# A transformer block on one core: products with the values issued for two attention steps together, and a third buffer of exponentials

## The reference

```python
c6 = silu(c) @ Wc + bc                     # shift, scale, gate for each half
xm = modulate(ln(x), sh_msa, sc_msa)
q, k, v = xm @ Wq + bq, xm @ Wk + bk, xm @ Wv + bv     # split into 16 heads
w = softmax(q / 16 @ k^T)                  # 512 x 512 per head
x = x + g_msa * ((w @ v) @ Wo + bo)
h = gelu(modulate(ln(x), sh_mlp, sc_mlp) @ W1 + b1)    # exact gelu
x = x + g_mlp * (h @ W2 + b2)
```

## Time and profile before

| | |
|---|---|
| median of three runs | 863.87 us (856.36 to 866.10) |
| span of the profiled execution | 857.3 us; its own time is not listed beside it |
| mean granted TensorE clock | 0.906 |
| TensorE matmuls busy | 725.0 us, 85% |
| VectorE busy | 582.5 us, 68% |
| ScalarE busy | 384.3 us, 45% |
| GpSimd busy | 222.2 us, 26% |
| maxima of the score blocks (L895) | 335.9 us, 512 times |
| exponentials (L497) | 247.9 us, 256 times |
| score blocks (L594) | 201.5 us, 512 times |
| transposed scores (L624) | 156.9 us, 512 times |
| products with the values (L616) | 137.3 us, 1024 instructions |

### The profile page before, as it was taken

The page is one execution under the profiler, slowest core; times in us unless marked ns, Lnnn a source line. Parts: engine busy times, 40 slices in busy tenths (PEclk is TensorE's granted clock), DMA queues, the critical chain, the costliest instruction groups (busy, mean ns, idle before and its releaser), DMA issues.

```text
span 857.3 us, 11761 instructions
## 1 busy us (share of the span) xinstructions
PE 725.0 (85%) x3967; PEld 390.6 (46%) x3967; DVE 582.5 (68%) x1015; ACT 384.3 (45%) x462; POOL 222.2 (26%) x163
## 2 busy tenths in 40 slices
PE   4648589865999599995999599997999798999987
PEld 1531122422247432682257522682258422851776
DVE  5728588863987488874987388875987587560373
ACT  0410156303763177423763167424762376269321
POOL 4262001200316103430315103430325030331244
PEclk9775599956999899997999799998999899899998
DMA  7499700295018910395028910393028611111210
GB/s 262 121 122 161 117 14 26 95 160 94 25 52 152 143 53 25 125 136 113 26 70 143 138 52 25 129 145 100 26 88 148 107 45 36 43 63 37 65 31 24
DMA packets 68774, 75.87 MB, mean 88 GB/s; under 512 B 6214, under 2 KB 59996, under 8 KB 68716
## 3 DMA queue, kind: packets, MB, share of 16 engines
q1 hardware_dynamic: 68716, 75.10, 43.5%
HBM read 49.35 MB, written 25.48 MB: 87 GB/s over the span
## 4 chain that ended last, share of the span: by engine, by line
issue 36%; PE 30%; DVE 11%; POOL 10%; DMA 7%; SPq 3%; ACT 2%; POOLq 0%; DVEq 0%; ACTq 0%
PE ps L616 6%; PE ps L594 6%; PE ps L624 5%; DVE mx L895 5%; PE ps L549 4%; POOL hl L442 4%; PE ps L755 3%; DMA qst<-mrow 3%; SPq L322 3%; DMA kst<-parts_scratch 2%; POOL prob L435 2%; PE ps L759 2%; ACT prob L497 1%; POOL x L415 1%; POOL xd L428 1%
## 5 line engine op out<-in xcount | busy, mean ns | idle before, releaser
L895 DVE TENSOR_REDUCE mx<-ps 128x1 f32<-128x512 f32 x512 | 335.9, 686 | 83.8 <-PE ps L594 80.0
L497 ACT ACTIVATE prob<-ps 128x1024 f32<-128x1024 f32 x256 | 247.9, 1022 | 237.4 <-PE ps L624 237.0
L594 PE MATMUL ps<-kst,qst 96*128 96x512 bf16 x512 | 201.5, 417 | 33.9 <-DVE mx L895 17.5
L624 PE MATMUL ps<-qst,kst 98*128 98x512 bf16 x512 | 156.9, 402 | 60.6 <-DMA qst<-mrow 52.9
L594 PEld LDWEIGHTS ps<-kst,qst 96*128 96x128 bf16 x512 | 46.1, 99 | 204.0 <-DVE mx L895 166.7
L616 PE MATMUL ps<-prob,vaug 128*32 128x512 f32 x1024 | 137.3, 608 | 0.4 <-ACT prob L497 0.3
L442 POOL TENSOR_TENSOR hl<-z,hh 128x512 fp32r<-128x512 f32 x64 | 82.3, 1286 | 138.6 <-DVE hh L1024 138.6
L624 PEld LDWEIGHTS ps<-qst,kst 98*128 98x128 bf16 x512 | 48.8, 102 | 130.1 <-DMA qst<-mrow 54.2
L536 ACT ACTIVATE z<-ps,bias_t 128x512 f32<-128x512 f32 x64 | 44.0, 688 | 135.7 <-PE ps L759 130.1
L390 POOL TENSOR_TENSOR rstd<-vare,mhalf 128x4 f32<-128x4 f32 x16 | 16.3, 1021 | 330.4 <-DVE vare L835 330.4
L549 PE MATMUL ps<-w_hi,hh 128*128 128x256 f32 x256 | 73.6, 287 | 0.3 <-POOL hl L442 0.3
(11 more groups left out here) (106 smaller groups left out, 858.6 us busy)
## 6 DMA issues: line engine op xcount, KB each, us to landing
parts_scratch<-prob SPq DMA_DIRECT2D x32, 384.0 KB, 2.6
qst<-parts_scratch SPq DMA_DIRECT2D x48, 256.0 KB, 11.2
kst<-parts_scratch SPq DMA_DIRECT2D x48, 256.0 KB, 17.6
y_scratch<-rb SPq DMA_DIRECT2D x32, 256.0 KB, 2.0
xa<-in_x_dram SPq DMA_DIRECT2D x8, 512.0 KB, 9.4
xd<-in_x_dram SPq DMA_DIRECT2D x8, 512.0 KB, 3.5
yc<-y_scratch SPq DMA_DIRECT2D x16, 256.0 KB
rb<-r_scratch SPq DMA_DIRECT2D x16, 256.0 KB
```

The lines of the kernel that those rows point to most:

```text
L497: act.activation(prob[:, s % 2, 2 * p:2 * p + 2, :], ps[:, 2 * p:2 * p + 2, :], ACT.Exp, scale=1.0 / DH).then_inc(exp_done, 1)
L594: pe.matmul(ps[:, banks[n % len(banks)], :], qst[1 - par][0:MROW, h, t * P:(t + 1) * P], kst[1 - par][0:MROW, h, :], start=True, stop=True ...
L624: m = pe.matmul(ps[:, q, :], kst[par][0:KROWS, G * g + q, kt * P:(kt + 1) * P], qst[par][0:KROWS, G * g + q, :], start=True, stop=True)
L895: dve.tensor_reduce(mx[:, t, h:h + 1], ps[:, banks[n % len(banks)], :], AXX, ALU.max).then_inc(max_done, 1)
```

## The change

The products of steps s - 2 and s - 1 are issued together, in odd steps s. Even steps issue none, and have four score blocks, two behind each half of the transposed scores; odd steps have two, one behind each half, and none behind the products (steps 14 and 15 keep four each). In pass 0 each step keeps four blocks, in two pairs. The exponentials have three places, s % 3: the two of `prob`, and a third laid over `z` and `yc`; an exponential of step s waits for the products of step s - 3. The copy out of PSUM moves from steps 5, 9, 13 to steps 6, 10, 14. `gbias` gets a buffer of its own, and the values' buffer of odd items has 17 columns a head (16 values and a one) instead of 32.

```diff
--- before.py
+++ after.py
@@ -46,7 +46,7 @@
 QK_BANKS = (4, 5, 2, 3)
 
 
-C_BLOCKS = (1, 0) + (3,) * (STEPS - 4) + (4, 4)
+C_BLOCKS = (1, 0) + (4, 2) * ((STEPS - 4) // 2) + (4, 4)
 TURN_BLOCKS, QK_BLOCKS, V_BLOCKS = (1, 1), (0, 1, 0, 1), (0, 1, 0, 1)
 UP_BLOCKS, DOWN_BLOCKS = (1, 1, 1), (2, 2, 2, 2, 2, 0, 0, 0)
 assert sum(map(sum, (C_BLOCKS, TURN_BLOCKS, QK_BLOCKS, V_BLOCKS, UP_BLOCKS, DOWN_BLOCKS))) == NH * TT
@@ -104,7 +104,7 @@
 
         stage = qst[1][:].rearrange("p h s -> p (h s)").bitcast(F32).rearrange("p (n f) -> p n f", n=2)
         mlp_stage = kst[1][:].rearrange("p h s -> p (h s)").bitcast(F32)
-        vaug = [sb(f"vaug{n}", [P, TT, NH, 2 * DH]) for n in (0, 1)]
+        vaug = [sb(f"vaug{n}", [P, TT, NH, width]) for n, width in enumerate((2 * DH, DH + 1))]
         wc_half = [vaug[0][:].rearrange("p t h d -> p (t h d)")[:, 0:6 * H],
                    qst[0][:].rearrange("p h s -> p (h s)").bitcast(F32)[:, 0:6 * H]]
 
@@ -124,13 +124,15 @@
 
         ga = sb("ga", [P, H])
         gm = sb("gm", [P, H])
-        gbias = yc[:, 0, 0:H]
+        gbias = sb("gbias", [P, H])[:]
         xd = sb("xd", [P, TT, H])
         x1 = sb("x1", [P, TT, H])
         hb = z1
         hh = sb("hh", [P, HR, S], F32R)
         hl = sb("hl", [P, HR, S], F32R)
         osb = xn[1]
+        prob_bufs = tuple([prob[:, n, q, :] for q in range(G)] for n in range(2)) + ([z1[:, 0, :], z1[:, 1, :], yc[:, 0, :], yc[:, 1, :]],)
+        prob_pairs = tuple([prob[:, n, 2 * p:2 * p + 2, :] for p in range(2)] for n in range(2)) + ([z1[:], yc[:]],)
 
 
         c_loaded, wc_loaded, bc_loaded, bias_loaded = sem("c_loaded"), sem("wc_loaded"), sem("bc_loaded"), sem("bias_loaded")
@@ -490,13 +492,13 @@
                     for s in range(STEPS):
                         for p in range(2):
                             act.wait_ge(st_done, 32 * i + 2 * s + p + 1)
-                            if s >= 2:
-                                act.wait_ge(pv_done, STEPS * i + s - 1)
+                            if s >= 3:
+                                act.wait_ge(pv_done, STEPS * i + s - 2)
                             elif later(i, 0, 1):
                                 act.wait_ge(pv_done, STEPS * i)
-                            act.activation(prob[:, s % 2, 2 * p:2 * p + 2, :], ps[:, 2 * p:2 * p + 2, :], ACT.Exp,
+                            act.activation(prob_pairs[s % 3][p], ps[:, 2 * p:2 * p + 2, :], ACT.Exp,
                                            scale=1.0 / DH).then_inc(exp_done, 1)
-                        if s >= 5 and s % TT == 1:
+                        if s > TT and s % TT == 2:
                             evacuate_y(i, s // TT - 1)
                 if runs(i, 2):
                     if not later(i, 2, 1):
@@ -613,7 +615,7 @@
                     elif later(b, 0, 1):
                         pe.wait_ge(x1_gated, b)
                 for q in range(G):
-                    m = pe.matmul(ps[32 * q:32 * q + 32, 4 + g % 2, :], vaug[par][:, kt, G * g + q, :], prob[:, s % 2, q, :],
+                    m = pe.matmul(ps[32 * q:32 * q + vaug[par].shape[3], 4 + g % 2, :], vaug[par][:, kt, G * g + q, :], prob_bufs[s % 3][q],
                                   start=kt == 0, stop=kt == TT - 1, skip_group_check=True)
                 m.then_inc(pv_done, 1)
 
@@ -660,12 +662,13 @@
                                 pe.wait_ge(exp_done, 32 * i + 2 * s - 1 + p)
                                 transposed_scores(i, par, s, p)
                             if later(i, 0, 1):
-                                between(p, p + 1)
+                                between(*((0, 2), (2, 4))[p] if s % 2 == 0 else (p, p + 1))
                             elif p == 1:
                                 between(0, 2)
-                        if s:
-                            pv(i, par, s - 1)
-                        between(2, old + new)
+                        if s % 2:
+                            for turn in range(max(s - 2, 0), s):
+                                pv(i, par, turn)
+                        between(4 if later(i, 0, 1) and s % 2 == 0 else 2, old + new)
                         if s == OLD_TURN and not later(i, 0, 1):
                             turn_maxima(i - 1, NH // 2, NH)
                     pe.wait_ge(exp_done, 32 * (i + 1))
```

## The result

The changed kernel takes 901.35 us (median of 4 runs, 892.11 to 903.67) against 864.99 for the kernel before (4 runs, 856.36 to 866.49). The ratio is 1.042, 95% interval 1.037 to 1.047: 36 us more, where 42 more and 906 were forecast. The profiled execution took 901.82 us with a span of 900.0; the two profiled spans differ by 42.7 us. The stretch at 395 to 439 us that the rows ahead of the prediction call item 2 is that of item 3, counted from 0; the code is the same for both.

What follows compares the result with a forecast made beforehand. TensorE's order of matmuls and products was taken to bound the steady steps. Items 1 to 5 +28.4, item 6 +4.5, item 0 +3.4 and item 7 +5.7 made +42 on 863.9: 906 us, range 884 to 923.

Steps and rivals of the forecast that it cites:

- What bounds the kernel: Steady attention steps of 2.62 us: TensorE's matmuls and products fill the step; waits for maxima cost nothing.
- The products, -0.24 a pair: Products of two steps issued together save 0.24 us a pair of steps; the bounds were 0.10 and 0.24.
- The score blocks, +0.69: Items 1 to 6, even steps: third and fourth score blocks wait for maxima, 0.30 and 0.39 us, +0.69 a pair.
- the walk: Start-by-start timing of a pair of attention steps; in items 1 to 6 without pieces, 5.68 us against 5.24 before.
- The pieces, +0.49 to +0.60 in an even step: LayerNorm pieces on VectorE delay even steps' maxima: +0.60 us for two, +0.49 for the variance; free in odd steps.
- The exponentials don't bind: Attention, ScalarE: the half that the odd step overwrites is free at 1.73 us, before 2.42; third buffer's waits cost nothing.
- Item 7, +5.7: Last item, without score blocks: next scores wait behind 1.86 us of joined products; a pair takes 5.09 us, +5.7 in all.
- Edits without a price: Bias buffer, later copy of y, third buffer over z and yc, and 17-column values: taken as 0.
- Rival 1: LayerNorm pieces cost nothing in VectorE's slack, only the blocks' stalls count: 889 us, 13%.
- Rival 2: Maxima are ready for the even step's blocks, so saved change-overs win 13.4 us: 850 us, 10%.
- Rival 3: Joined products are dearer, no batch following in 0.43 us across steps, and queued maxima follow every 0.66: 919 us, 14%.
- Rival 4: The 17-column products don't run side by side: 165 us more; 3% together with anything further.

Runs made afterwards that it cites:

- experiment 5: Each maximum over half of the 512 keys: kernel before 824.66 us, changed kernel 845.84; the latter with odd-step blocks behind the first half of scores 836.08.
- experiment 2: Changed kernel with products issued in each step again, score blocks left at four and two: 896.26 us, ratio 1.039 to the kernel before.
- in 1: Changed kernel with three score blocks in each step again, products still joined: 886.29 us, ratio 1.022 to the kernel before.
- in 4: Changed kernel with three blocks a step, LayerNorm pieces in odd steps and item 7's products in each step: 880.07 us, ratio 1.016 to the kernel before.
- the memory alone: Kernel before plus only the change's third buffer, waits, 17 columns, bias buffer and later copy of y, old order: 856.82 us, ratio 0.990; again 859.80, 0.991.
- experiment 3: Two separate edits of the changed kernel: LayerNorm pieces moved to odd steps, 883.48 us (1.019 to before); item 7's products in each step again, 895.63 us (1.036).

## Why the prediction was right, point by point

**What bounds the kernel.** Right. TensorE's written order bounds the steps; experiment 5 shows it from the other side, since steps stay at 2.62 us with quick maxima. It holds for the steady steps alone: item 0 and the stretches outside the attention got shorter with them.

**The products, -0.24 a pair.** Right in size: 5.90 against 5.67 us with the same blocks, 0.23. The other bound, 0.10, is out. The third and fourth batch follow as the second does.

**The score blocks, +0.69.** Right: 0.66 from experiment 2, with the two waits at the walk's places. The weight load waited each time (438.84, 439.44), and no later matmul passed the waiting block: the scores behind block d start at 439.67. The Trainium skill (TensorE: Matmul & The Clock Gate, Part 2) says that matmuls stay in program order, and this trace agrees. VectorE was through with the pair's maxima at +4.63 (438.10 + 3.77, less 437.24); the walk's 4.9 is a slip, since its own terms give 3.92 + 0.68 = 4.60, and nothing hangs on it.

**The pieces, +0.49 to +0.60 in an even step.** Right: pairs of 6.20 and 6.28 us, and 2.91 us of item 3 returned when they were moved.

**The exponentials don't bind.** Right for the kernel as changed, whose odd step's second scores come at 3.09 us (440.33 less 437.24), but for a reason that I had half: only the first half was checked. The second half's trip ends at 2.70, as the walk of item 7 even says. This gap made my forecasts of later experiments too low: by 0.4 us a pair without pieces in 1, by 0.4 a pair in 4, and by 0.3 in 5.

**Item 7, +5.7.** Measured 5.2; a pair takes 5.01 and not 5.09 us, since ScalarE's first round trip is 1.72 there and not 1.78.

**Edits without a price.** Wrong in sign, by a little: the memory alone gains 0.9%. This is the term that was mis-sized. The order costs 43.1 us in the trace's attention, and with some 7 us less from the memory the medians' 36 come out. That is arithmetic over different runs, and the profile didn't locate those 7 us. Other kernels bear it out: in the changed kernel, in experiments 1 to 4 and in both runs of the memory kernel, the median lies 6 to 9 us lower, set against that of the kernel before, than its attention alone would put it. The half-maximum kernels go the other way (21.2 us between them, 14.1 in the attention), from two runs each. A gain outside the attention would account for the 5 us between 906 and the measured time, and a change there is what the prediction itself had named as a sign of being wrong. One part has a small price: item 7 took 33.8 us with the memory alone, against 33.6 before and 33.5 with 17 columns alone. In its trace the copy of y, moved to step 14, stands before the last step's exponentials.

**The rivals.** Rival 1 (pieces free) fell by experiment 3 and by the pairs of 6.28 us. Rival 2 (change-overs win) fell twice: blocks c and d do wait 0.30 and 0.38 us, and with quick maxima in the same order the pair is 5.31. Rival 3 (dearer joined products) fell by the 0.23, and queued maxima followed every 0.60 to 0.62 us (six in 3.77 at 438.10). Rival 4 fell: 17-column products run four at a time, in 0.43 us a batch.

## What to carry to other kernels

Before issuing a long block of work at once on an in-order engine, ask what it was covering where it stood: here one microsecond of products in each step covered both VectorE's maxima and ScalarE's round trip, and joined in the odd step it left the even step bare. Walk a period through the rows, with every buffer's round trip in it and not only the first; the walk gave the pairs of items 1 to 6 within 0.03 us, and the one trip left out cost the forecasts that depended on it 0.3 to 0.4 us a pair. When the last stage of a pipeline lacks one kind of work, look at it separately: item 7 lost 5 us for a reason of its own.

## What the runs showed of the hardware

Products of 17 columns of fp32 weights ran four side by side in their quarters like those of 32, at about the same 0.60 us each (means in the changed kernel 0.60 and 0.62; weight loads 0.10 against 0.11). A maximum over 256 instead of 512 columns took 0.42 instead of 0.68 us. The kernel with the memory alone gained 0.9%, with pairs of 5.22 to 5.24 us in the stretch that was edited, where they took 5.24 before, and this stays open.
